# Reordered stage boundaries in a six-sublayer decoder kernel: first loads, drains, and a transpose

## The reference

```
x = LN(x + gated_linear_attention(x))      # 4 heads, low-rank decay gates
x = LN(x + cross_attention(ctx, x))        # softmax over the queries
x = LN(x + quantised_ffn(x))               # 128 -> 512 -> 128, rounded operands
x = LN(x + causal_alibi_attention(x))      # softmax over the keys
x = LN(x + masked_cross_attention(x, ctx)) # softmax over the keys
x = LN(x + mixture(x))
# mixture: x @ base_w.T + base_b
#          + 2 * sum_{e,r} (x @ lora_A)[r] * softmax(x @ router_w.T + router_b)[e] * lora_B[e, r]
```

## Time and profile before

| | |
|---|---|
| median of 3 runs | 1536.48 us (1534.01 to 1548.83) |
| the profiled execution's own time | 1530.52 us |
| its span, first to last instruction | 1528.6 us |
| mean granted TensorE clock | 0.943 of full speed |

### The profile page before, as it was taken

How to read it: one execution, slowest core, us unless ns; L and a number is a source line. 1 busy time by engine, 2 the same in 40 slices (tenths; PEclk the granted TensorE clock), 3 DMA queues, 4 the chain that set the end, 5 groups by cost and what they waited for, 6 DMA issues and landing times.

```text
span 1528.6 us, 63791 instructions
## 1 busy us (share of the span) xinstructions
PE 1284.3 (84%) x26566; PEld 845.9 (55%) x26566; DVE 1213.7 (79%) x2629; ACT 1050.6 (69%) x2244; POOL 803.5 (53%) x1590
## 2 busy tenths in 40 slices
PE   5788888899876777776666679999999999999897
PEld 2455555566544444444333346767766666666685
DVE  2546666776546888888799979999999999999865
ACT  2446566677555788887677767777777777777655
POOL 2455465666655787877788853334433233332233
PEclk9789799999887899997899999999999999999999
DMA  7000000000000000000000000000000000000012
GB/s 199 15 3 3 2 3 3 3 4 3 3 9 9 24 17 24 17 17 17 2 2 1 2 2 3 3 3 3 3 3 10 18 18 23 17 17 17 2 43 70
DMA packets 28671, 24.28 MB, mean 16 GB/s; under 512 B 3676, under 2 KB 23906, under 8 KB 28386
## 3 DMA queue, kind: packets, MB, share of 16 engines
q1 hardware_dynamic: 28386, 20.21, 4.8%
HBM read 15.94 MB, written 4.19 MB: 13 GB/s over the span
## 4 chain that ended last, share of the span: by engine, by line
PE 40%; POOL 24%; issue 20%; DVE 9%; ACT 6%; SPq 0%; DMA 0%; POOLq 0%; DVEq 0%; ACTq 0%
PE keys_T L590 8%; PE keys_O L571 5%; POOL gla_low L1156 4%; PE keys_O L577 4%; PE keys_E L485 3%; PE keys_S L331 3%; POOL gla_yg L1186 3%; POOL cross_pairs L837 3%; POOL gla_gate L1179 2%; POOL cross_spread L804 2%; PE keys_E L528 2%; DVE ffn_hh L2011 2%; ACT keys_pT L657 2%; POOL gla_sq L1173 2%; PE keys_O L597 2%
## 5 line engine op out<-in xcount | busy, mean ns | idle before, releaser
L340 POOL TENSOR_SCALAR keys_spread<-keys_kT,keys_heads 128x512 f32<-128x512 f32 x128 | 87.0, 699 | 229.1 <-ACT keys_kT L621 229.1
L657 ACT ACTIVATE keys_pT<-keys_T 128x512 f32<-128x512 f32 x256 | 152.5, 596 | 76.5 <-PE keys_T L590 73.1
L350 DVE TENSOR_REDUCE keys_mx<-keys_S 128x16 f32<-128x1024 f32 x128 | 156.3, 1221 | 15.5 <-PE keys_S L331 13.9
L590 PE MATMUL keys_T<-ident_sb,keys_pexp 128*128 128x128 f32 x1024 | 164.9, 284 | 3.2 <-ACT keys_pT L657 2.3
L353 DVE TENSOR_TENSOR keys_pe_in<-keys_S,keys_mx 128x1024 f32<-128x1024 f32 x128 | 156.8, 1225 | 4.4
L590 PEld LDWEIGHTS keys_T<-ident_sb,keys_pexp 128*128 128x128 f32 x1024 | 112.3, 141 | 72.3 <-ACT keys_pT L657 38.4
L673 ACT ACTIVATE keys_pexp<-keys_pe_in 128x1024 f32<-128x1024 f32 x128 | 134.8, 1053 | 0.1
L710 DVE RECIPROCAL keys_rinv<-keys_O 128x128 f32<-128x128 f32 x128 | 120.5, 941 | 0.1
L1631 DVE COPY_PREDICATED gla_at<-gla_node,gla_GP 128x256 f32<-128x256 int32 x128 | 65.2, 510 | 57.8 <-ACT gla_at L1483 54.4
L1156 POOL TENSOR_TENSOR gla_low<-gla_ex,gla_kT 128x128 f32<-128x128 f32 x160 | 72.0, 482 | 54.4 <-ACT gla_ex L1474 54.4
L571 PEld LDWEIGHTS keys_O<-keys_pT,keys_vz 128*32 128x32 f32 x4096 | 63.0, 109 | 64.5 <-ACT keys_pT L657 64.1
(11 more groups left out here) (290 smaller groups left out, 3767.8 us busy)
## 6 DMA issues: line engine op xcount, KB each, us to landing
context<-in_ctx_T SPq DMA_DIRECT2D x32, 256.0 KB, 2.7
xs<-in_x SPq DMA_DIRECT2D x8, 512.0 KB, 7.1
out_x<-xs SPq DMA_DIRECT2D x16, 256.0 KB, 2.3
keys_mask_q<-keys_mask_b SPq DMA_DIRECT2D x64, 1.0 KB
keys_bias_right_f<-in_alibi_right SPq DMA_DIRECT2D x1, 512.0 KB, 3.8
ffn_w<-in_L_ffn_w_gate_T SPq DMA_DIRECT2D x1, 256.0 KB, 4.8
ffn_w<-in_L_ffn_w_up_T SPq DMA_DIRECT2D x1, 256.0 KB, 5.0
ffn_w<-in_L_ffn_w_down_T SPq DMA_DIRECT2D x1, 256.0 KB, 5.9
```

The lines of the kernel that those rows point to most:

```text
L350: nc.vector.tensor_reduce(m, quads(S), X, ALU.max).then_inc(c["mx"], 1)
L590: last = nc.tensor.transpose(T[:, j * P:(j + 1) * P], pexp[:, t % 2, (4 * half + j) * P:(4 * half + j + 1) * P], sh.ident[:, :])
L657: nc.scalar.activation(pT[:, t % 2, 4 * half:4 * half + 4, :].rearrange("q n k -> q (n k)"), T[:, :], ACT.Copy).then_inc(c["pT"], 1)
```

## The change

Four edits:

1. The loads of `gla` are split. SyncE issues `ident`, `b3`, `wg1`, `wg2` (a new semaphore `first`), the first eighth of `x`, and `rms`, `decay`, `node`; ScalarE issues the five projection loads before its table load. SyncE then waits until all `weights` of `gla` have landed before it issues the loads of `ffn` and everything after. TensorE and VectorE begin on `first`; the wait for `weights` and `scaled` stands ahead of the first `queries`, and VectorE scales `wq` and `wout` after the bias split.
2. `Part` has a new number `leads`. In the first `leads` slots of a stage the new stage's slot is issued ahead of the old stage's drain slot instead of behind it. It is 2 for `ffn` on TensorE, ScalarE and VectorE, and 0 (as before) everywhere else.
3. VectorE's `logits(0)` and `gates(0)` of the mixture move from `body(-1)` into `body(0)`, behind the last `keys` drain slot.
4. TensorE's outer-product step uses `transpose` instead of `matmul`, and bias and base product move ahead of it in `body(g)`.

```diff
@@ sequence
-                if before and n < before.lag:
+                if before and part.leads <= n < before.lag:
                     before.slot(before.groups * G + n)
                 for h, half in enumerate(part.halves):
                     half(g, g % 2, t)
+                    if before and n < part.leads:
+                        before.slot(before.groups * G + n)
@@ gated_linear_attention
-        loads = [(wg1[:, :], a["Wgk1"]), (wg2[:, :], a["Wgk2_T"]),
-                 (b3[:, :], a["bgk2"].rearrange("(a n) -> a n", a=1).to_broadcast([3, D])),
-                 (wq[:, :], a["Wq_T"]), (wk[:, :], a["Wk_T"]), (wvg[:, 0:VW], a["Wv_T"]), (wvg[:, VW:], a["Wg_T"]),
-                 (wout[:, :, :], a["Wout_T"].rearrange("(f q) n -> q f n", f=2)),
-                 (rms[0:GDV, :], a["rms_w"].rearrange("(q a) -> q a", a=1)),
+        b.first_loads = [(b3[:, :], a["bgk2"].rearrange("(a n) -> a n", a=1).to_broadcast([3, D])),
+                         (wg1[:, :], a["Wgk1"]), (wg2[:, :], a["Wgk2_T"])]
+        b.projections = [(wq[:, :], a["Wq_T"]), (wk[:, :], a["Wk_T"]), (wvg[:, 0:VW], a["Wv_T"]),
+                         (wvg[:, VW:], a["Wg_T"]), (wout[:, :, :], a["Wout_T"].rearrange("(f q) n -> q f n", f=2))]
+        loads = [(rms[0:GDV, :], a["rms_w"].rearrange("(q a) -> q a", a=1)),
...
+        stage.loaded = lambda eng: eng.wait_ge(c["weights"], NW)
+
+        def load_first(sp):
+            for dst, src in b.first_loads:
+                sp.dma_start(dst, src).then_inc(c["first"], 16)
@@ tensor, gla
-            pe.wait_ge(c["weights"], NW)
+            pe.wait_ge(c["first"], NF)
...
-            pe.wait_ge(c["scaled"], 2)
...
             def queries(g, p):
+                if g == 0:
+                    pe.wait_ge(c["weights"], NW)
+                    pe.wait_ge(c["scaled"], 2)
@@ scalar, gla
+            for dst, src in b.projections:
+                act.dma_start(dst, src).then_inc(c["weights"], 16)
             nc.scalar.preload_act_table_set("natural_log_exp_and_others")
@@ vector, gla
-            dve.wait_ge(c["weights"], NW)
+            dve.wait_ge(c["first"], NF)
...
+            dve.wait_ge(c["weights"], NW)
+            nc.vector.tensor_scalar(wq[:, :], wq[:, :], float(GDK) ** -0.5, None, ALU.mult).then_inc(c["scaled"], 1)
+            nc.vector.tensor_scalar(wout[:, :, :], wout[:, :, :], rms[:, 0:1], None, ALU.mult).then_inc(c["scaled"], 1)
@@ quantised_ffn, the parts of tensor, scalar and vector
-            return Part(early, (slot,), 2, parts=G, prepare=prepare)
+            return Part(early, (slot,), 2, parts=G, prepare=prepare, leads=2)
@@ lora_mixture, tensor
-                    last = nc.tensor.matmul(OT[:, i * TILE:(i + 1) * TILE],
-                                            outer[:, p, 2 * i:2 * i + 2, :].rearrange("q t n -> q (t n)"),
-                                            sh.ident[:, :], start=True, stop=True)
+                    last = nc.tensor.transpose(OT[:, i * TILE:(i + 1) * TILE],
+                                               outer[:, p, 2 * i:2 * i + 2, :].rearrange("q t n -> q (t n)"),
+                                               sh.ident[:, :])
...
             def body(g):
                 if live(g):
+                    base(g)
                     turn_outer(g, g % 2)
                 if g + 3 < NG:
                     turn_x(g + 3)
                 if live(g):
-                    outputs(g, g % 2)
+                    experts(g, g % 2)
@@ lora_mixture, vector
             def body(g):
-                if live(g + 1):
+                if g == 0:
+                    logits(0)
+                    gates(0, 0)
+                if g >= 0 and live(g + 1):
                     logits(g + 1)
                 if live(g - 1):
                     residual(g - 1, (g - 1) % 2)
-                if live(g + 1):
+                if g >= 0 and live(g + 1):
                     gates(g + 1, (g + 1) % 2)
@@ decoder, sync
                 sp.dma_start(sh.ident[:, :], d["ident"]).then_inc(sh.consts, 16)
+                gla.load_first(sp)
+                load(0)
                 gla.load(sp)
-                load(0)
+                gla.loaded(sp)
                 ffn.load(sp)
                 keys.load(sp)
```

More of the change, by code:

```diff
@@ L122, with __init__ @@
 class Part:
-    def __init__(self, early=None, halves=(), lag=0, parts=2 * G, groups=NG, body=None, drain=None, prepare=None):
+    def __init__(self, early=None, halves=(), lag=0, parts=2 * G, groups=NG, body=None, drain=None, prepare=None,
+                 leads=0):
+        self.leads = leads
         self.early, self.halves, self.lag, self.parts = early, halves, lag, parts
@@ L1087, in gated_linear_attention @@
         c = Counts(sh, nc, "gla")
-        c.new("weights", "zeros", "split", "scaled", "wz_done", "wz",
+        c.new("first", "weights", "zeros", "split", "scaled", "wz_done", "wz",
               "xT_done", "xT", "z_done", "za", "ze", "zl", "g", "q_done", "qT", "k_done", "kT",
@@ L1094, in gated_linear_attention @@
         ZEROS = 4
-        loads = [(wg1[:, :], a["Wgk1"]), (wg2[:, :], a["Wgk2_T"]),
-                 (b3[:, :], a["bgk2"].rearrange("(a n) -> a n", a=1).to_broadcast([3, D])),
-                 (wq[:, :], a["Wq_T"]), (wk[:, :], a["Wk_T"]), (wvg[:, 0:VW], a["Wv_T"]), (wvg[:, VW:], a["Wg_T"]),
-                 (wout[:, :, :], a["Wout_T"].rearrange("(f q) n -> q f n", f=2)),
-                 (rms[0:GDV, :], a["rms_w"].rearrange("(q a) -> q a", a=1)),
+        b.first_loads = [(b3[:, :], a["bgk2"].rearrange("(a n) -> a n", a=1).to_broadcast([3, D])),
[3 more added lines that the diff above has]
+        loads = [(rms[0:GDV, :], a["rms_w"].rearrange("(q a) -> q a", a=1)),
                  (rms[GDV:P, :], a["rms_w"].rearrange("(q a) -> q a", a=1)),
                  (decay[:, :], sh.dram["decay_sums"]), (node[:, :], sh.dram["node_mask"])]
-        NW = 16 * len(loads)
+        NF, NW = 16 * len(b.first_loads), 16 * (len(loads) + len(b.projections))
         def span(level):
@@ L1138, in gated_linear_attention @@
         stage.normed = lambda eng, g: eng.wait_ge(c["norm"], (g + 1) * G)
+        stage.loaded = lambda eng: eng.wait_ge(c["weights"], NW)
+        def load_first(sp):
+            for dst, src in b.first_loads:
+                sp.dma_start(dst, src).then_inc(c["first"], 16)
+        stage.load_first = load_first
         @stage.on("gpsimd")
@@ L1577, in _ @@
         def _(dve):
-            dve.wait_ge(c["weights"], NW)
+            dve.wait_ge(c["first"], NF)
             dve.wait_ge(sh.consts, 16)
             nc.vector.tensor_copy(cut0[:, :], b3[:, :]).then_inc(c["split"], 1)
-            nc.vector.tensor_scalar(wq[:, :], wq[:, :], float(GDK) ** -0.5, None, ALU.mult).then_inc(c["scaled"], 1)
             dve.wait_ge(c["split"], 1)
             nc.vector.tensor_tensor(rest1[:, :], b3[:, :], cut0[:, :], ALU.subtract).then_inc(c["split"], 1)
-            nc.vector.tensor_scalar(wout[:, :, :], wout[:, :, :], rms[:, 0:1], None, ALU.mult).then_inc(c["scaled"], 1)
             dve.wait_ge(c["split"], 2)
@@ L1956, in slot @@
                     normalise(n[0], n[1])
-            return Part(early, (slot,), 4, parts=G)
+            return Part(early, (slot,), 4, parts=G, leads=2)
         @stage.on("vector")
@@ L2066, in slot @@
                     moments(out[0], out[1])
-            return Part(early, (slot,), 4, parts=G, prepare=prepare)
+            return Part(early, (slot,), 4, parts=G, prepare=prepare, leads=2)
         return stage
@@ L2195, in turn_outer, with base @@
                 for i in range(2):
-                    last = nc.tensor.matmul(OT[:, i * TILE:(i + 1) * TILE],
-                                            outer[:, p, 2 * i:2 * i + 2, :].rearrange("q t n -> q (t n)"),
-                                            sh.ident[:, :], start=True, stop=True)
+                    last = nc.tensor.transpose(OT[:, i * TILE:(i + 1) * TILE],
+                                               outer[:, p, 2 * i:2 * i + 2, :].rearrange("q t n -> q (t n)"),
+                                               sh.ident[:, :])
                 last.then_inc(c["outerT_done"], 1)
-            def outputs(g, p):
+            def base(g):
                 if g < 2:
@@ L2212, in outputs, with experts @@
                                      start=False, stop=False)
+            def experts(g, p):
+                out = OUT[g % 2]
                 c.await_nth(pe, "outerT", g, 1, 1)
```

## The result

Measured beside each other, the kernel before took 1539.57 us and the changed one 1523.82 (medians of four runs, ratio 0.9885, 95% interval 0.9849 to 0.9921). Twelve runs each in two later measurements gave 0.9966 (0.9933 to 0.9999) and 0.9963 (0.9929 to 0.9998), with medians of 1529.86 and 1529.76 us. So the change is faster, by 0.3 to 0.4% in the larger measurements, whose intervals just leave out 1, and not by the 1% of the first. Executions over 1.5% slower than their kernel's fastest are left out of all ratios and fits (22 of the 310 in the later measurements), and the two profiles among them, the second one of the changed kernel and the one of edit 2 alone, are read for their first 40 us only. The forecast of 1531.6 us had the direction right, but the first measurement came 7.8 us under it, with three times the 4.9 us of gain; the later ones put the gain by their ratios at 5 to 6.

A forecast was written before the change was run, and what follows sets the result against it. No single engine bounds the kernel (PE busy 84%, DVE 79%); an edit is worth what it takes from the chain at its place. +0.4 - 0.8 - 1.9 - 2.6 = -4.9, so 1536.5 - 4.9 = 1531.6 us; range 1522 to 1540.

The forecast's parts named there:

- Head up to the first transposes: Start of `gla`: PE begins transposing `x` at 7.8 us in place of 12.5, -4.7 us.
- The first fetch waits behind the bulk: PE's stop in `gram`: instruction fetch waits for bulk loads, PE resumes at 36.7 us, lead spent; head worth +0.4 us.
- The rule named in the prediction: DMA queues, `gram`: engine goes round queue rows packet by packet, so a fetch would pass within a fraction of a microsecond.
- SyncE's wait: SyncE ahead of the `ffn` loads: new wait for the weights makes all of the bulk 0.4 us late.
- rival B: SyncE's new wait: weights land at 12.5 us, bulk late by 4.9 us, slower, +2.3 in sum, 1538.8 us; chance 0.10.
- Part 2: End of `cross`: first `ffn` tile ahead of the drain, -0.8 us, bounds -2.0 and +2.0.
- Part 3: End of `keys`: drained ahead of the router, `mix` starts 1.9 us earlier, bounds -3 and 0.
- The bound of 0: End of `keys`: nothing gained if the router, now late, is last in its turn.
- Part 4: `mix`: two transposes replace four matmul passes, saving 0.26 us less 0.1 wait per period; -2.6 us, bounds 0 and -4.2.
- The sum: Whole kernel: +0.4 head, -0.8 end of `cross`, -1.9 end of `keys`, -2.6 `mix`, giving -4.9 us.
- Rival A: Head: the first instruction fetch isn't held up, so -4.7 us is kept; sum -10.0, 1526.5 us; chance 0.27.
- The caution that `gla`'s later stops would stay equal: `gla`: the sum holds the later stops' length constant; a change in their length would show the forecast wrong.

## Why the prediction was right and wrong

- **Head up to the first transposes: right, a little too good.** 4.7 us forecast, 5.2 in the profile (12.51 to 7.29), but 4.0 on average: they start at 11.94 to 12.51 us in nine profiles with the old head and at 7.29 to 8.43 in eight with the new one. In the profile shown the bias split and not `x` was last, which the text had ruled out; in six of the eight `x` is last, as forecast.
- **"The first fetch waits behind the bulk": wrong.** This is the step that failed: edit 1 was put at +0.4 us, its whole lead spent in a stop of 8.9 us, where the stop was 2.50 and edit 1 alone gave -4.7. The reading of the earlier trace rows was one late packet that started as the rate fell, and the fall was a coincidence: in later profiles of the same head the packet starts anywhere from 31.1 to 33.6 us, the early ones under full rate. What stands in its place is shown by taking the bulk away: it delays the packet by 1.4 and 1.7 us in the two heads, so the term cancels between before and after. What sets the size of this delay is open. The rule named in the prediction, that a DMA engine goes round its queue rows packet by packet, as the Trainium skill (DMA: Bandwidth & Descriptors, Queues, rings and completion order) has it, leaves no room for a wait until the bulk's end, and the traces agree (25.95 us, amid 285 GB/s). "Within a fraction of a microsecond" was my conclusion from it, and is too good by some 1.5 us.
- **SyncE's wait (rival B): too low, and without effect.** 0.4 us forecast; the bulk went out 0.36 us later in the profile shown (7.99 against 7.63) and 0.9 to 1.4 later in the others, and no later time shows it.
- **Part 2: right in the trace,** 0.7 us for 0.8, and too small to be seen in the end time (-0.1, 1.5 either way). The prediction calls VectorE the busiest engine but for PE from 720 to 740 us; the earlier trace rows has GpSimd at 12.60 us and VectorE at 11.58. The term does not use it.
- **Part 3: half.** The 1.6 us ahead of the last product came (1.7). What the sum left out is that the router is then last: PE stands 0.99 us for `outer`. In the profile 1.0 us is left of 1.9 (from the last exponential to the second copy of `outerT` 16.4 us before, 15.4 after); without edit 4 nothing is. Beside edit 4 it is more: with edit 4 and without edit 3 the second copy comes at 17.3 in both profiles, so edit 3 takes 1.9 us off there, which about repays what the new order costs. The bound of 0 had named the router as last.
- **Part 4: mechanism right, size short.** 0.16 us per period forecast, 0.21 in the trace, with the wait of 0.1 us just as put; the two transposes take 0.22 us from step to step and not 0.26. At the end -5.5 us (1.5 either way) were measured for 2.6, of which the period explains 3.4 at most. The term left out that the new order delays the first group, which works the other way; the rest of the 5.5 is open.
- **The sum.** -4.9 forecast, -8.2 (1.1 either way) measured at equal half-clock time: 5 us too little for the head, about 1 us too little for `mix`, 2 to 3 too much for the stage ends. That 4.9 lies near the 5 to 6 us of the later ratios is luck: the errors went against each other, and the changed kernel's runs happened to spend more time at half clock. Rival A's sum of -10.0 had the right head and the same excess at the stage ends. The range held all three medians. The caution that `gla`'s later stops would stay equal was the right one to give: they don't, but they differ as much between two executions of one kernel.

## What to carry to other kernels

When a stop coincides with a change in traffic, one instance is no cause: move the traffic and see whether the stop moves with it. Where run time scatters with PE's clock, compare kernels at equal time at half clock; here that cut the scatter from 5.6 us to 2.2 and let 5 us be told apart with twelve runs. And before a wait or a load is moved behind another, look for who stands in line behind it on every engine: a mask that is used 800 us later cost 9 us because its preparation was early in VectorE's stream.

## What was not expected of the hardware

- PE runs out of instructions 19 to 23 times in `gla`, most of them 510 to 514 matmuls and weight loads apart, for 0.4 to 3.3 us each (the first for up to 4.7), 31 to 36 us in all. A fetch is a 16 KB packet of 0.9 to 1.5 us, and PE goes on 2.2 to 3.0 us after the packet starts, with and without traffic beside it.
- A full-rate bulk of 290 GB/s delays the start of such a packet by some 1.5 us on average, 2.6 at most, with one profile for each head to stand for no bulk.
- One us at half clock costs 0.32 us of run time in this kernel, and the same binary spends 158 to 235 us there.
- Two transposes in float32 take 0.22 to 0.26 us from step to step where four matmul passes take 0.52, and the profiles show no more time at half clock with them.
